# A graph network on one core: edge weights moved into VectorE's masks, TensorE fed from the gather ring, and a shorter SyncE step in the attention

## The reference, cut to what matters

```python
def _conv(x, row, col, edge_type, edge_weight, W, b):      # row = src, col = dst
    deg_inv_sqrt = where(deg > 0, deg ** -0.5, 0)           # deg counts col
    norm = deg_inv_sqrt[row] * deg_inv_sqrt[col] * edge_weight
    xw = einsum('ni,tio->tno', x, W)
    x_j = xw[edge_type, col] * norm[:, None]
    return leaky_relu(segment_sum(x_j, row) + b, 0.01)
z1 = _conv(x, ...); z2 = _conv(z1, ...); z3 = _conv(z2, ...)
x = layernorm(x + (x + z1 + z2 + z3) / 4)
# then attention with 2 heads of 64: per edge a leaky relu of two scores,
# a softmax over the edges of one dst, and the weighted sum of xp[src]
x = layernorm(x + attention(x))
```

## Time and profile before

| | |
|---|---|
| ordinary runs | 8935.12, 8934.26, 8933.91 us; median 8934.26 us |
| span of the profiled execution | 12163.5 us |
| busy, of the profiled span | GpSimd 6376.4 us (52%), TensorE 5878.0 (48%), VectorE 4437.4 (36%), ScalarE 4089.9 (34%) |
| chain that ended last | ScalarE's instruction stream 30%, issue 27%, VectorE 12%, ScalarE 8%, TensorE 5% |
| mean granted TensorE clock | 0.610 |

### The profile page before, as it was taken

The page is one execution under the profiler, slowest core; times in us unless marked ns, Lnnn a source line. Parts: engine busy times, 40 slices in busy tenths (PEclk is TensorE's granted clock), DMA queues, the critical chain, the costliest instruction groups (busy, mean ns, idle before and its releaser), DMA issues.

```text
span 12163.5 us, 152908 instructions
## 1 busy us (share of the span) xinstructions
PE 5878.0 (48%) x30961; PEld 4676.7 (38%) x30962; DVE 4437.4 (36%) x11587; ACT 4089.9 (34%) x12236; POOL 6376.4 (52%) x6521
## 2 busy tenths in 40 slices
PE   6844434434533444343534434343455555555555
PEld 4632322323322323232323323232355555555554
DVE  9952222222322222222312222221455555555556
ACT  6522222222322222222312222222344445445445
POOL 1656565565456565656466565656344444444443
PEclk9965555555655555555655555555566666666666
DMA  1011111111231111111211111111122222222222
GB/s 47 34 43 42 39 43 42 39 43 39 61 57 43 38 43 39 42 38 43 73 42 42 38 42 39 42 39 43 42 72 69 68 68 70 69 69 69 68 69 64
DMA packets 432692, 612.47 MB, mean 50 GB/s; under 512 B 232038, under 2 KB 249491, under 8 KB 432539
## 3 DMA queue, kind: packets, MB, share of 16 engines
q0 software_dynamic: 208832, 428.96, 13.9%
q1 hardware_dynamic: 223707, 182.02, 4.6%
HBM read 437.29 MB, written 51.28 MB: 40 GB/s over the span
## 4 chain that ended last, share of the span: by engine, by line
ACTq 30%; issue 27%; another core or an unknown queue 14%; DVE 12%; ACT 8%; PE 5%; DVEq 3%; POOL 0%; DMA 0%; SPq 0%; POOLq 0%
ACTq L893 9%; ACTq L891 9%; ACTq L906 9%; ACT g_step L906 8%; ACTq L904 2%; DVEq L1597 2%; DVE a_miss L1710 2%; ACTq L903 1%; PE bank L1190 1%; DVE a_msg L1761 1%; DVE a_max L1715 1%; DVE lo_hot L1255 1%; PE wide L1190 1%; DVE acc L1781 1%
## 5 line engine op out<-in xcount | busy, mean ns | idle before, releaser
L732 POOL DMA_INDIRECT g_rows<-gcn_table,rec_idx x4743 | 4474.9, 943 | 3125.2 <-ACT g_step L906 1707.4
L906 ACT ACTIVATE g_step<-g_rows,rec_w 128x128 f32 x5580 | 1904.4, 393 | 5800.3 <-issue 4599.8
L1190 PE MATMUL bank<-g_step,g_hot 128*128 128x128 f32 x7440 | 1750.1, 409 | 2431.0 <-ACT g_step L906 1377.0
L1190 PEld LDWEIGHTS bank<-g_step,g_hot 128*128 128x128 f32 x7440 | 1504.2, 300 | 2815.9 <-issue 2815.9
L757 POOL DMA_INDIRECT a_roll<-gat_table,src_plane x1612 | 1520.8, 943 | 1815.1 <-ACT a_cand L931 1344.2
L1627 DVE TENSOR_TENSOR acc<-acc,bank 128x512 f32 x930 | 638.3, 686 | 4137.2 <-remote 2732.6
L1190 PE MATMUL wide<-g_step,g_hot 128*128 128x128 f32 x3720 | 869.1, 407 | 1038.3 <-issue 507.0
L1225 PE MATMUL bank<-a_pair,a_hotT 128*128 128x4 f32 x3608 | 647.7, 303 | 1225.5 <-DVE a_pair L1792 1208.4
L1190 PEld LDWEIGHTS wide<-g_step,g_hot 128*128 128x128 f32 x3720 | 747.5, 299 | 1228.6 <-issue 1228.6
L1225 PEld LDWEIGHTS bank<-a_pair,a_hotT 128*128 128x128 f32 x3608 | 660.0, 273 | 1256.2 <-DVE a_pair L1792 1238.0
L931 ACT ACTIVATE a_cand<-a_miss,a_rows 128x128 f32<-128x128 bf16 x3608 | 1095.9, 386 | 39.1 <-DMA a_rows<-a_roll 27.3
(11 more groups left out here) (269 smaller groups left out, 5166.1 us busy)
## 6 DMA issues: line engine op xcount, KB each, us to landing
a_rows<-a_roll SPq DMA_DIRECT2D x451, 264.0 KB
g_rows<-gcn_table,rec_idx POOLq DMA_INDIRECT x4743
gcn_table<-rows SPq DMA_DIRECT2D x147, 256.0 KB
a_roll<-gat_table,src_plane POOLq DMA_INDIRECT x1612
e_dst<-by_dst_dst SPq DMA_DIRECT2D x451, 2.0 KB
gat_table<-acc SPq DMA_DIRECT2D x7, 462.0 KB
out_x<-xs SPq DMA_DIRECT2D x6, 448.0 KB
gcn_slots<-nothing SPq DMA_DIRECT2D x4, 468.0 KB, 6.8
```

Of the source, the lines that this page charges most:

```text
L732: pool.indirect_dma_start(out=g_rows[:, tile % RING, :], out_offset=None, in_=gcn_tables[layer % 2], in_offset=bass.IndirectOffsetOnAxis(a ...
L906: last = nc.scalar.activation(g_step[:, j, k, :].unsqueeze(1), g_rows[:, bass.ds(slots[k], 1), :], ACT.Copy, scale=rec_w[:, bass.ds(q.at(0 ...
L1190: last = nc.tensor.matmul(sums_of(j)[:, bass.ds(places[k], D)], g_hot[:, j % 3, k, :], g_step[:, j % 3, k, :], start=False, stop=(k == GP ...
```

## The change

In the layers the weight goes into the mask: VectorE makes each of the four masks with an operation of its own, (iota is equal to rec_lo) times rec_w, so rec_lo becomes float32. ScalarE's scaled copies go, and with them g_step and s_copied. TensorE multiplies the masks with the ring's rows directly: it loads five values per group, each of four holding slot and place in one number, waits for the landing itself, and splits the numbers by shift and mask. GpSimd's waits for the ring are for TensorE's finished groups (s_gpe). The lists are laid out anew for this. In the attention the destinations are loaded once, as a plane dst_plane in 13 transfers in layer 2, beside the one of the sources; SyncE's step loads one register and issues one transfer; VectorE loads its two blocks and the group of the step five ahead with one load of three numbers.

```diff
-        rec_lo = sb("rec_lo", [P, SLOT_TILES], BF16, gcn_scope)
+        dst_plane = sb("dst_plane", [P, GAT_GROUPS * GAT.tiles])
+        rec_lo = sb("rec_lo", [P, SLOT_TILES], F32, gcn_scope)
-        g_step = sb("g_step", [P, 3, GP, D], F32, gcn_scope)
-        e_dst = sb("e_dst", [P, R, T])
...
-            for n in range(CSPANS):
-                sp.dma_start(planes[:, n, :, :], groups[n]).then_inc(s_src, 16)
+            for k, plane in enumerate((src_plane, dst_plane)):
+                groups = by_dst[k][0:EDGES_PAD, 0].rearrange("(n g p t) -> n p g t", n=CSPANS, p=P, t=GAT.tiles)
+                planes = plane[:, :].rearrange("p (n g t) -> p n g t", n=CSPANS, t=GAT.tiles)
+                for n in range(CSPANS):
+                    sp.dma_start(planes[:, n, :, :], groups[n]).then_inc(s_src[k], 16)
...
             def body(q):
-                if q.live(2):
-                    group = sp.value_load(gat_at[0:1, bass.ds(q.at(2), 1), 0], min_val=0, max_val=GAT_GROUPS - 1)
-                    if q.live(2 - R):
-                        wait_apart(sp, sa["cand"], q.at(2 - R, 1, 1), s_apart)
-                    sp.dma_start(e_dst[:, q.slot(2), :].unsqueeze(1), dst_groups[:, bass.ds(group, 1), :]
-                                 ).then_inc(s_el[q.slot(2)], 16)
                 if q.live(0):
-                    tile = sp.value_load(gat_at[0:1, bass.ds(q.at(0), 1), 0], min_val=0, max_val=GAT_GROUPS - 1)
-                    slot = sp.value_load(gat_at[0:1, bass.ds(q.at(0), 1), 1], min_val=0, max_val=ROLL - 1)
+                    _, (group,) = nc.values_load_multi_w_load_instructions(
+                        gat_at[0:1, bass.ds(q.at(0), 1)], engines=(mybir.EngineType.SP,), min_val=0,
...
-                    wait_apart(sp, s_land, tile + (3 * CH * CCOLS + 1), s_apart)
+                    wait_apart(sp, s_land, (group & GROUP_MASK) + (3 * CH * CCOLS + 1), s_apart)
...
-                            wait_apart(pool, s_copied, layer * GRP.steps - (-steps // GP), s_apart)
+                            wait_apart(pool, s_gpe, layer * GRP.steps - (-steps // GP), s_apart)
...
-                def scale(q, values):
-                    j = q.slot(0) % 3
-                    *slots, tile = values
-                    if q.live(-3) or layer:
-                        act.wait_ge(s_gpe, q.at(-3, 1, GRP.steps * layer + 1))
-                    act.wait_ge(s_land, tile + (CH * CCOLS * layer + 1))
-                    for k in range(GP):
-                        last = nc.scalar.activation(g_step[:, j, k, :].unsqueeze(1),
-                                                    g_rows[:, bass.ds(slots[k], 1), :],
-                                                    ACT.Copy, scale=rec_w[:, bass.ds(q.at(0, GP, k), 1)])
-                    last.then_inc(s_copied, 1)
...
-                def add_up(q, places):
+                def add_up(q, values):
                     j = q.slot(0)
+                    tile = values[GP] & TILE_MASK
...
                     pe.wait_ge(s_ghot, q.at(0, 1, GRP.steps * layer + 1))
-                    pe.wait_ge(s_copied, q.at(0, 1, GRP.steps * layer + 1))
+                    pe.wait_ge(s_land, tile + (CH * CCOLS * layer + 1))
                     for k in range(GP):
-                        last = nc.tensor.matmul(sums_of(j)[:, bass.ds(places[k], D)], g_hot[:, j % 3, k, :],
-                                                g_step[:, j % 3, k, :], start=False, stop=(k == GP - 1))
+                        slot, place = values[k] >> SLOT_SHIFT, values[k] & (GP - 1) * D
+                        last = nc.tensor.matmul(sums_of(j)[:, bass.ds(place, D)], g_hot[:, j % 3, k, :],
+                                                g_rows[:, bass.ds(slot, 1), :].rearrange("p g d -> p (g d)"),
+                                                start=False, stop=(k == GP - 1))
...
-                        lo = rec_lo[:, bass.ds(q.at(2, GP), GP)]
-                        V.tensor_tensor(g_hot[:, j, :, :], spread(iota_ps.unsqueeze(1), [P, GP, P]),
-                                        spread(lo.unsqueeze(2), [P, GP, P]), ALU.is_equal).then_inc(s_ghot, 1)
+                        for k in range(GP):
+                            step = bass.ds(q.at(2, GP, k), 1)
+                            last = V.tensor_scalar(g_hot[:, j, k, :], iota_ps, rec_lo[:, step], rec_w[:, step],
+                                                   ALU.is_equal, ALU.mult)
+                        last.then_inc(s_ghot, 1)
...
+                _, (b, b2, group) = nc.values_load_multi_w_load_instructions(
+                    gat_turn[:, bass.ds(q.at(LO_AHEAD), 1), :].rearrange("p i k -> p (i k)"),
+                    engines=(mybir.EngineType.DVE,), min_val=0, max_val=GAT_GROUPS - 1,
...
-                    b, = blocks_of(gat_block[0:1, bass.ds(q.at(2), 1)])
...
-                    b2, = blocks_of(gat_block[0:1, bass.ds(q.at(-2), 1)])
...
-                    dve.wait_ge(s_el[l], q.landed(5))
-                    V.tensor_scalar(a_lo[:, l, :], e_dst[:, l, :],
-                                    gat_base[:, bass.ds(q.at(5), 1)], None, ALU.subtract).then_inc(sa["lo"], 1)
+                    V.tensor_scalar(a_lo[:, l, :].unsqueeze(1), dst_of[:, bass.ds(group, 1), :],
+                                    gat_base[:, bass.ds(q.at(LO_AHEAD), 1)], None, ALU.subtract).then_inc(sa["lo"], 1)
```

More of the change, by code:

```diff
@@ L387, in gnn_kernel @@
         s_gtw = sem("s_gtw")
-        s_el = [sem(f"s_el{k}") for k in range(R)]
         sa = {n: sem(f"sa_{n}") for n in ("lo", "miss", "cand", "T", "hotT", "scale", "node", "p", "msg",
@@ L714, in _ @@
                 if layer:
-                    pool.wait_ge(s_copied, layer * GRP.steps)
+                    pool.wait_ge(s_gpe, layer * GRP.steps)
                 for q in range(SORT.steps):
@@ L881, in body @@
                         gat_rows(n - 1)
-                    if 0 <= n < NBATCH and layer == 2:
+                    if n < NBATCH and layer == 2:
                         ln_sqrt(n, BATCHES[n])
@@ L1022, in list_begun @@
                 for c in range(CH):
-                    last = nc.tensor.matmul(begun_blocks[:, c, :], ones[0:NB, 0:65], ended[:, c, :],
+                    last = nc.tensor.matmul(begun_blocks[:, c, :], ones[0:NB, 0:33], ended[:, c, :],
                                             start=True, stop=True)
@@ L1174, in places_of @@
                 def places_of(q):
-                    _, places = nc.values_load_multi_w_load_instructions(
-                        gcn_at[64:65, bass.ds(q.at(0), 1), 0:GP].rearrange("p g k -> p (g k)"),
-                        engines=(mybir.EngineType.PE,), min_val=0, max_val=(GP - 1) * D,
-                        skip_runtime_bounds_check_because="a block less its group's first, at most one per step")
-                    return places
-                def add_up(q, places):
+                    _, values = nc.values_load_multi_w_load_instructions(
+                        gcn_at[32:33, bass.ds(q.at(0), 1), :].rearrange("p g k -> p (g k)"),
+                        engines=(mybir.EngineType.PE,), min_val=0, max_val=(RING - 1) * GP * D,
+                        skip_runtime_bounds_check_because="a slot of the ring, and a block less its group's first")
+                    return values
+                def add_up(q, values):
                     j = q.slot(0)
+                    tile = values[GP] & TILE_MASK
                     if q.live(-3) or layer:
@@ L1568, in list_tiles @@
+                chain(V.tensor_tensor(by_group(off), by_group(at),
+                                      spread(by_group(at)[:, :, 0:1], [1, CSTEPS // GP, GP]), ALU.subtract))
                 dve.sem_inc(s_count, 1)
-                chain(V.tensor_scalar(row_no[0:33, :], row_no[0:33, :], float(c * CCOLS + CCOLS - 1), None, ALU.min))
-                chain(V.tensor_scalar(row_i[0:33, :], row_no[0:33, :], 705.0, None, ALU.mult))
-                tile_row = row_no[32:33, :].rearrange("p (g k) -> p g k", k=GP)
@@ L1576, in list_tiles @@
+                V.tensor_copy(groups_of[:, c, :, GP], by_group(row)[:, :, GP - 1])
+                chain(V.tensor_scalar(turn, turn, 16, None, ALU.logical_shift_right))
+                chain(V.scalar_tensor_tensor(at, turn, -float(RING), row, ALU.mult, ALU.add))
+                chain(V.scalar_tensor_tensor(groups_of[:, c, :, 0:GP], by_group(at), float(GP * D), by_group(off),
                                              ALU.mult, ALU.add))
@@ L1580, in _ @@
                 list_tiles(c)
-            chain(V.tensor_scalar(gat_block[:, :], gat_base[0:1, :], 1.0 / P, None, ALU.mult))
-            chain(V.tensor_tensor(gat_group[:, :], iota_n[0:1, 0:GAT.groups], gat_block[:, :], ALU.subtract))
-            chain(V.tensor_scalar(gat_group[:, :], gat_group[:, :], float(GAT_GROUPS - 1), None, ALU.min))
-            chain(V.tensor_copy(gat_at[:, :, 0], gat_group[:, :]))
-            chain(V.tensor_scalar(gat_at[:, :, 1], gat_at[:, :, 0], ROLL - 1, None, ALU.bitwise_and))
```

(15 more changed lines are left out.)

100 lines of the change are left out of this document (42 added, 58 removed).

## The result

The kernel after takes 9119.58 us (median of 4 runs, 9118.4 to 9122.36), the kernel before 8934.63 us in the same series. The ratio is 1.0207, interval 1.0195 to 1.0219: **185 us slower**, where no change was forecast.

The account below looks back on a forecast made before the run. The prediction took POOL's string of gathers as the bound before and after (66%). Terms: -4 us for ScalarE's copies, +3 for masks at layer ends, 0 elsewhere; sum -1, so 8933 us, range 8880 to 8960.

Parts of the forecast that it names:

- The step that failed: Attention, VectorE's register loads: one load of three adds about +0.1 us on 3.9, so the step stays under POOL's 4.46.
- The room: Attention: POOL leaves 4.46 us a step, ScalarE's candidates start 3.88 us apart when catching up, so 13% to spare.
- the recording is what slows the engines: Whole kernel: recording slows engines with many small instructions, explaining a profiled span 3229 us longer than the ordinary median.
- the sum: Whole kernel before: gathers at 1.248 us (8047 us), plus sorting and gaps, give 9160 us without waits, 226 over the median.
- The sign that the profiled span would fall by 500 us or more: Profile after: ScalarE nearly idle in the layers, so recording slows less; span falls some 500 us, ordinary time stays.
- The masks: VectorE, layers: four masks at 0.26 us, +0.36 per group; hidden in stages, +3 us behind layers 1 and 2, 0 before attention.
- ScalarE's copies: Layers: removing the copies gives 0 in the stages and -4 us behind the three layers' last gathers; bounds 0 and -5.
- TensorE on the ring, the later release: Layers: TensorE's group grows to 3.15 us, under 4.99, and slots come free about 2.5 us later; both cost 0.
- rival B: Start of layer 1: decoding ends after POOL's 93 free slots are used, exposing +18 us; 8952 to 8968 us; 12%.
- The port: VectorE and GpSimd, SBUF: the new masks read an iota in PSUM, so they do not hold up the gathers.
- rival C: Layers: masks block GpSimd though they read PSUM; +0.077 us per gather, +372 us, 9306 us; 4%.
- Rival A: POOL's waits for ScalarE are not all recording; up to about 100 us faster, 8834 at most, 8880 in the middle; 18%.

Follow-up runs that it names:

- load_behind_max: The kernel after with only VectorE's load of three registers moved behind the issue of a_max: 8947.27 us, ratio 1.0014; on another chip 8956.41 us, ratio 1.0015.
- before_third: The kernel before, unchanged, run for a profile; it met a chip of the slower group: 12152.08 us.

## Why the prediction was wrong

It said 8933 us, 8880 to 8960; 9120 is outside, and none of its rivals is what happened.

**The step that failed** is this one: "VectorE's two loads of one register become one of three, about +0.1 us on 3.9: the step stays under 4.46." It priced the load and not its place. Before, both loads were issued behind a_max and ran beside its 1.22 us; their time was in no step. After, 0.75 us of load stand between a_lo and a_max, +0.8 us on a quick step and not +0.1, and most steps around 8000 us take 4.67 to 4.92 us. VectorE took over from POOL: 4.84 and not 4.46 us a step, (4.84 - 4.46) x 451 = 171 us, of which 141 lie in the stage and 31 behind it. The room was taken too large as well. The 3.9 is right for the quickest steps: load_behind_max has 3.90, 3.91 and 3.95 us where VectorE catches up, against the 3.88 us of the earlier trace rows. But the mean step with the load hidden is about 4.1 us by the estimate above, so the room was some 0.37 us (8%) and not 0.56 (13%). With 0.56 the bare load would have cost (0.75 - 0.56) x 451 = 86 us, half of what it did. The bounds of -3 and +3 for the attention came from naming GpSimd alone; the moved instruction was in the diff, and a rival "the load is bare" would have given 0.7 to 0.8 us a step.

**What bounds the kernel**: right, though the argument beside it was wrong. POOL's string of gathers is the bound in the first kind's profile of before: intervals of 1.25 us in all stages, no wait for the ring. But "the recording is what slows the engines" has fallen. The ordinary runs of before took 12152 to 12232 us on one group of chips, too. The warning was in the sum: 9160 us with not one wait, 226 over the median. It was put down to recording once more. The gaps of the earlier trace rows were those of the second kind: 95, 95, 137 and 93.5 us there, 28.9, 27.8, 61.6 and 65.1 on the first. There the closing batches are under way before the last gather (layer 1: first z at 2661.8 us, last gather at 2710.8), on the second kind they begin behind it (3287.3 and 3268.2 in before_third). These four differences are 237 us, all of the excess. The sign that the profiled span would fall by 500 us or more came true (12163.5 to 9120.1 us) by luck: the two profiles are of different kinds. On one kind the span rose.

**The masks**: taken at 0.26 us each, measured 0.402 (0.34 in a row), above the upper bound of 0.393 taken singly; per group +0.68 us, inside the bounds of +0.21 and +0.89. In the stages they are hidden, as said. At the ends of layers 1 and 2 the forecast of +3 stands against +0.6 for both gaps. Before the attention "VectorE waits about 1 us in each, so 0" failed: +0.68 a batch, +7.7 us.

**ScalarE's copies**: their removal was to give -4; nothing of it can be seen. That the shorter path in the gaps was paid back by masks is possible and not shown.

**TensorE on the ring, the later release**: right at 0. The wait at the start of layer 1 (rival B; the 47.25 us of the earlier trace rows) doesn't exist on the first kind: from 760 to 899 us neither before nor load_behind_max has a gap between gathers, so the rival's condition never held. The layers' half was slower all the same, by 11 us, and elsewhere.

**The port** (rival C): refuted. The gather in the layers takes 946 ns beside the new masks, 947 before; the 1.40 us of the earlier trace rows stay with the list code. The iota that they read lies in PSUM. By the rule of the Trainium skill (SBUF — State Buffer, Who interferes with whom) a VectorE operation with at most one input in SBUF, outside the two-port modes, doesn't contend with GpSimd. The trace agrees, 946 against 947 ns.

**Rival A**: refuted with the reading it rested on. On the first kind ScalarE held up nobody, and on the second, where POOL waits 1680 us for g_step, the change didn't bring time either: its chain goes through TensorE (29%), issue (33%) and the unknown wait (12%) where it went through ScalarE's stream.

What stays open: what causes the pauses of the second kind, and whether it belongs to the chip; the 9 us that the attention takes longer behind the new layers; the 3.9 us of the tail.

## What to carry to other kernels

A register load costs its place before its length: here it was free behind the issue of a long operation, and at the head of a step, between the last and the first operation, its whole length was added to the step. When a step has little room, work out each moved instruction of its stream against that room, and take the room from the mean step and not from the quickest. Past it another engine becomes the bound. And if the profiled span and the ordinary times differ by a third, they may not be of one kind: an argument on rooms and gaps needs a profile whose span is that of the times.

## What the runs showed of the hardware

Two groups of chips: the same program takes 8935 to 8943 us on one and 12152 to 12232 us on the other, with equal durations of ScalarE's copy (386 and 387 ns) and the gather (947 and 946), and on the other pauses of mostly 6 to 12 us near to once in three steps of VectorE's loop in the attention. VectorE's register loads from SBUF: 0.30, 0.53 and 0.75 us for one, two and three; hidden beside a tensor_reduce of 1.22 us, and added to the step (+0.34, +0.61 and +0.79 us for one register, two loads of one, and one of three) where nothing runs beside them. A 128x128 tensor_scalar from PSUM to SBUF with two scalars takes 0.402 us, 0.34 in a row, against 0.683 us for a tensor_tensor of four times the size.
